# Later places in the order for the steps of ScalarE and VectorE that read a projection, the transposed maxima and the mixed values

## The reference

```
x = x + 0.5 * _L0_ffn_ref(_layernorm(x))    # 8 experts of 256, top 2, squared relu
x = x +       _L0_attn_ref(_layernorm(x))   # 32 heads of 32, output layer norm
x = x + 0.5 * _L0_ffn_ref(_layernorm(x))
x = x + 0.5 * _L1_ffn_ref(_layernorm(x))    # 8 experts of 512, top 2, capacity 640
x = x +       _L1_attn_ref(_layernorm(x))   # 16 heads of 64, biases on q, k, v
x = x + 0.5 * _L1_ffn_ref(_layernorm(x))
```

## Time and profile before

| | |
|---|---|
| median of three runs | 3482.12 us |
| the profiled execution, its own time | 3475.47 us |
| its span, first to last instruction | 3473.7 us |
| TensorE busy over the span | 3046.4 us (88%) |
| TensorE's weight loads | 1900.0 us (55%) |
| VectorE / ScalarE / GpSimd busy | 2161.3 / 1726.7 / 1745.8 us |
| mean granted clock of TensorE | 0.941 of full speed |

### The profile page before, as it was taken

How to read it: one execution, slowest core, us unless ns; L and a number is a source line. 1 busy time by engine, 2 the same in 40 slices (tenths; PEclk the granted TensorE clock), 3 DMA queues, 4 the chain that set the end, 5 groups by cost and what they waited for, 6 DMA issues and landing times. The chain is left out here.

```text
span 3473.7 us, 46628 instructions
## 1 busy us (share of the span) xinstructions
PE 3046.4 (88%) x16106; PEld 1900.0 (55%) x16106; DVE 2161.3 (62%) x4520; ACT 1726.7 (50%) x3306; POOL 1745.8 (50%) x1540
## 2 busy tenths in 40 slices
PE   7999999999999999979862849999999999999276
PEld 6884455454545455458752835555555555554165
DVE  5567666676666666746666425666766666666642
ACT  5555666666666666646540414344443444433032
POOL 0005877788787878840101724444444435444056
PEclk9999999999999999989985969999999999999578
DMA  2004334333333333300010434433434444433034
GB/s 88 1 19 92 86 81 93 74 82 85 81 86 87 83 86 78 74 25 16 13 41 24 82 89 100 92 90 85 104 89 92 98 95 95 98 85 68 25 69 73
DMA packets 182987, 254.00 MB, mean 73 GB/s; under 512 B 35904, under 2 KB 75584, under 8 KB 182208
## 3 DMA queue, kind: packets, MB, share of 16 engines
q1 hardware_dynamic: 168672, 240.19, 29.3%
q0 software_dynamic: 14080, 10.82, 2.3%
HBM read 33.44 MB, written 16.67 MB: 14 GB/s over the span
## 5 line engine op out<-in xcount | busy, mean ns | idle before, releaser
L1737 POOL TENSOR_TENSOR arena<-arena 128x512 f32<-128x512 f32 x1152 | 1439.8, 1276 | 866.7 <-ACT arena L1119 843.4
L780 PE MATMUL psum<-stack 96*128 96x512 f32 (+4 forms) x4096 | 1345.8, 442 | 70.0 <-DMA stack<-halves 42.3
L1375 DVE TENSOR_REDUCE top<-psum 128x1 f32<-128x512 f32 x1536 | 1002.0, 685 | 406.0 <-PE psum L780 402.0
L1119 ACT ACTIVATE arena<-psum 128x512 f32<-128x512 f32 x1536 | 866.3, 595 | 449.6 <-PE psum L780 438.2
L780 PEld LDWEIGHTS psum<-stack 96*128 96x128 f32 (+4 forms) x4096 | 707.3, 191 | 676.3 <-issue 353.5
L810 PE MATMUL psum<-arena,values 128*32 128x512 f32 (+1 forms) x3072 | 552.8, 613 | 0.0
L1706 POOL TENSOR_SCALAR rstd<-mv 128x4 f32<-128x4 f32 x56 | 12.6, 226 | 581.7 <-DVE mv L1241 579.9
L768 PE MATMUL psum<-xT,wqkv 128*128 128x512 f32 x512 | 268.2, 605 | 6.7 <-DVE arena L1420 3.0
L1407 DVE RECIPROCAL psum<-psum 128x128 f32<-128x128 f32 x256 | 226.4, 926 | 61.6 <-PE psum L840 61.6
L1082 ACT ACTIVATE halves<-psum,bqk 128x512 fp32r<-128x512 f32 x128 | 87.9, 687 | 308.3 <-PE psum L768 308.3
L1327 DVE SCALAR_TENSOR_TENSOR X<-psum,weight,X 128x128 f32<-128x128 f32 x512 | 144.0, 344 | 143.4 <-PE psum L747 143.3
(11 more groups left out here) (154 smaller groups left out, 3064.7 us busy)
## 6 DMA issues: line engine op xcount, KB each, us to landing
stack<-halves SPq DMA_DIRECT2D x768, 128.0 KB, 2.3
stack<-halves SPq DMA_DIRECT2D x384, 256.0 KB, 4.8
tokens<-xn SPq DMA_DIRECT2D x16, 256.0 KB, 2.4
sums<-X SPq DMA_DIRECT2D x16, 256.0 KB, 3.4
wqkv<-in_wg SPq DMA_DIRECT2D x16, 256.0 KB
wqkv<-in_wu SPq DMA_DIRECT2D x16, 256.0 KB
wqkv<-in_wd SPq DMA_DIRECT2D x16, 256.0 KB
wqkv<-in_w_qkv SPq DMA_DIRECT2D x2, 1536.0 KB, 9.8
```

Of the source, the lines that this page charges most:

```text
L780: ins = T_.matmul(bk, st[0:k, side, slot + h, cols], st[0:k, 1 - side, slot + h, :], start=r == 0, stop=r == len(PARTS[l]) - 1)
L1119: S_.activation(prob[l][tile % N_PROB][:, h, :], psum[:, bank[key], :], ACT.Exp, scale=scale).then_inc(released[bank[key]], 1)
L1375: give(V_.reduce_max(top[i][:, j:j + 1], psum[:, bank[key], :], AX.X), key)
L1737: ins = G_.tensor_tensor(to[:, h, :], old[:, h, :], prob[l][tile % N_PROB][:, h, :], ALU.add)
```

## The change

It does four things, all of them to the order and none to the arithmetic.

1. The step `project` stays as it is for TensorE. What ScalarE does of it is now the step `high`, 0.06 of a group later than TensorE's; what VectorE and SP do is now `low`, 0.11 later in attention 0 and 0.10 in attention 1.
2. `rows` (the transposed maxima) has three calls, one for each reader: TensorE works at the first, ScalarE at the second, VectorE and SP at the third.
3. `mix` has one call more in attention 0: ScalarE's spread moves one call on (3.85 to 3.96), TensorE's transposes back and VectorE's multiplication with them (to 4.07 and 4.19).
4. Smaller: the copy of a transposed norm (`xT`) is a step `fill` of its own, about 0.06 later; routing has one call more; the copy of a group's weighted values (the second call of `last`) moves by 0.04 in attention 0.

```
 WHEN = (
-    dict(project=(-0.11, 0.67), maxima=(0.97, 1.82), rows=(1.85, 1.85), probs=(2.21, 3.17),
-         last=(3.18, 3.24), mix=(3.51, 4.19), out=(4.24, 5.01), ahead=(-2.20, -0.56),
+    dict(project=(-0.11, 0.67), high=(-0.05, 0.73), low=(0.00, 0.78), maxima=(0.97, 1.82), rows=(1.87, 1.96),
+         probs=(2.21, 3.17), last=(3.18, 3.32), mix=(3.51, 4.30), out=(4.24, 5.01), ahead=(-2.20, -0.56),
...
             queue("project", (l, n), 3, 3, n)
+            queue("high", (l, n), 3, 3, n)
+            queue("low", (l, n), 3, 3, n)
             queue("maxima", (l, n), heads * TILES_B, heads * TILES_B, n)
-            queue("rows", (l, n), 1, 1, n)
+            queue("rows", (l, n), 3, 3, n)
             queue("probs", (l, n), (heads + 1) * TILES_B - 1, (heads + 1) * TILES_B, n)
-            queue("mix", (l, n), 6, 6, n)
+            queue("mix", (l, n), 6 + (l == 0), 6 + (l == 0), n)
...
-            def project(l, n):
+            def high_halves(l, n):
...
             def rows_of_maxima(l, n):
                 i, n_top, key = n % 2, HEADS[l] * TILES_B, ("top", l, n)
+                yield
...
-            def project(l, n):
+            def low_halves(l, n):
...
-            def project(l, n):
+            def fill_stack(l, n):
                 s, hv, st, width = n % N_STACK, halves[n % 2], stack[n % N_STACK], WIDTH[l]
-                yield
                 yield
```

More of the change, by code:

```diff
@@ L1038, in ahead, with fill @@
                 yield from normalise(("a", l, b), b)
+                yield
+            def fill(l, b):
                 fill_xt(("a", l, b))
@@ L1209, in experts1 @@
                 yield
-            play(order, dict(load0=load0, prepare0=prepare0, route=route, ahead=ahead, compute0=compute0,
-                             project=project, rows=rows_of_maxima, probs=probabilities, last=last_tile, mix=mix,
+            play(order, dict(load0=load0, prepare0=prepare0, route=route, ahead=ahead, fill=fill, compute0=compute0,
+                             high=high_halves, rows=rows_of_maxima, probs=probabilities, last=last_tile, mix=mix,
                              settle=settle, experts1=experts1))
@@ L1911, in _ @@
                 load(X[:, b * TILES_B:(b + 1) * TILES_B, :], x_v[b], got_x[b])
-            play(order, dict(load0=load0, load_attention=load_attention, project=project, rows=rows_of_maxima,
+            play(order, dict(load0=load0, load_attention=load_attention, low=fill_stack, rows=rows_of_maxima,
                              route=route, keep=keep, experts1=experts1))
```

31 lines of the change are left out of this document (24 added, 7 removed).

## The result

The changed kernel takes 3716.10 us (median of four runs, 3706.25 to 3718.09) against 3482.28 us of the kernel before on the same chip (3475.59 to 3482.63): a ratio of 1.0675, with a 95% interval of 1.0655 to 1.0694, or +234 us. Forecast were 3606 us, in a range of 3530 to 3650. The sign was right, the size was not.

The account below looks back on a forecast made before the run. The prediction took TensorE's order and its waits in the two attentions as the bound. It added 71 + 54 + 6 = 131 us to the profiled 3475.5 us, giving 3606 us, in a range of 3530 to 3650.

Parts of the forecast that it names:

- Part 1: Attention 1: k's halves come later, so the DMA landing TensorE waits for is 1.42 us later in 50 groups: 71 us.
- Part 2: Attention 0, behind q: the spread stands in front of the exponentials, about 0.85 us in each of 64 groups: 54 us.
- Part 3: Attention 0: k's low half, 2.5 us later, fits into 2.9 of room; a score bank freed later costs 6 us.
- Part 4: Possible gains: 6.8 us before the norm's transposes, about offset; routing and `fill` 0; ScalarE's shorter waits worth only TensorE's share.
- rival C: Both attentions: waits of 2 to 3 us per group lower TensorE's clock, 66 us more, 3672 us; chance 0.05.
- Rival B: Both attentions: not slower, as engines take ready work first and free banks earlier; 3460 us; chance 0.08.

Follow-up runs that it names:

- e1: The kernel before with only the high and low halves of attention 1 placed later (0.18 and 0.22 instead of 0.12): 3576.03 us, ratio 1.0305.
- e4: The kernel before with only the seventh call of `mix` in attention 0: ratio 1.0115.
- e11: The kernel before with the seventh call of `mix` in attention 0 and `last` at 3.18 to 3.32 instead of 3.18 to 3.24: ratio 1.0144.
- e2: The kernel before with only routing's steps spread over seven calls instead of six: 3536.07 us, ratio 1.0193.
- e6: The changed kernel with routing back on six calls and the transposed maxima of attention 1 back at one place: 3651.88 us, ratio 1.0482.
- e13: The kernel before with routing on seven calls and GpSimd's additions cut from 512 to 16 columns in two groups per batch: 3512.44 us, ratio 1.0082.
- e5: The kernel before with late halves in attention 1, plus two useless matmuls ahead of each wait for the landings there: 3569.54 us, ratio 1.0252.

## Why the prediction was wrong in size

**Part 1, right in mechanism and in size.** In the groups with P first, which is what was read, the exponential, the high and the low half were forecast 1.08, 1.58 and 2.74 us behind the start of the ten matmuls and came at 1.08, 1.57 and 2.75. With M first the exponential waits for its product until 1.54 and the high half is at 2.03, and the low half is at 2.75 all the same: the high half and the reduction ahead of it end together, at 2646.80. The weight load waited for the landing in 52 groups (50 before). At full clock the landings cost 73 us by the groups of e1, forecast were 71. That the shift adds up so well is in part luck, since some positions lose 1.1 us and one 2.0. What e1 measured beyond it, 46 of its 119 us, is the clock.

**Part 2, right in size, wrong in place.** 54 + 6 were forecast, 67 measured. I numbered ScalarE's exponentials off by one against TensorE's products: the one that the third product needs runs ahead of the high half of q, not behind the spread. The weight load behind q waits 0.42 and no matmul a microsecond. Of the 67 us, 24 are in the one group of eight with the output norm, where ScalarE waits for the later multiplication. In a plain group `mix` brings 0.38 of 0.82 us (e4); TensorE waits 0.3 us for an exponential there. The rest comes with the copy of the weighted values and the high half of k, which stand ahead of exponentials in the row of ten (e11, and the rows of place 2). That the sum was close is luck: it was forecast as the same 0.85 us in each of 64 groups.

**Part 3, right.** The late low half of k went into its room: TensorE waits 1.1 us in two waits for `stack` in 300 to 1450.

**Part 4 has the first step that failed: "Routing and `fill` move by a twentieth of a group: 0".** It cost some 65 us, 51 in attention 1 and 14 in the experts (e2, and by the medians e6 the other way). The twentieth is `fill`'s, and I took it for both. The calls of routing stand 0.30 of a group apart before and after, and the last one, with nearly all of VectorE's routing work in it, moved by a whole call, from 6.40 to 6.70. Past what it moved I didn't look: it changed sides with the first reciprocal, whose multiplication gives a bank back to q. Nor did I look at what GpSimd does beside the new place: the call takes twice as long there, and e13 puts two thirds of the 51 us on that. What makes up the 14 us in the experts was not tried.

**The clock is the second: the sum has no term for it.** It stood only in rival C, with a chance of 0.05, as an alternative to the forecast, when it is an addition to it. Half clock in attention 1 rose from 23 to 181 us, and by the groups of e1 it cost 46 us there; rival C had priced it at 66. The sentence in the earlier trace rows that a stretch with waits of 0.7 has a clock of 1.00 was true, and says nothing of waits of 2 to 3 us.

**Rival B, not slower.** ScalarE's waits for q and k did shrink, from 277.9 us to 118.8 in attention 1. TensorE got nothing of it, as the prediction's objection to B says.

**The sum, as measured.** Attention 1: 73 (landings) + 46 (clock, with the landings late) + 51 (routing, with its own clock) = 170 taken singly, 159 in the profile of the changed kernel; the 11 us between lie within what single profiles differ by. Attention 0: 67. Experts: 18, of which routing 14. Together 243 us in the profiles, 234 by the medians. The forecast of 131 and the two terms it lacked, 65 and 46, make 242.

## What to carry to other kernels

Where the order comes from a table and each engine keeps to it, count an edit by what each moved step passes, not by how far it moves: three tenths of a group, past one reciprocal and into GpSimd's additions, cost 65 us. A rival can be an addition: the late landings brought waits, and the waits brought half clock. A filler against it has a price of its own, so read the clock's cost from groups at full and at half clock in one trace. And test the opposite edit: projections 0.05 to 0.13 of a group earlier took the wait away and made the kernel 27 us faster.

## What the runs showed of the hardware

- VectorE's operations with two fp32 operands in SBUF (128x256) take 0.42 us alone and 1.39 us while GpSimd adds 128x512 in SBUF, six in 8.10 us; a 128x32 one takes 0.19 and 1.19. Reductions of the same call (0.42) and those that read PSUM (0.69) don't change; one scaling with a single operand in SBUF does (0.17 and 0.96). The Trainium skill ("SBUF — State Buffer", SBUF: two separate sides) says that a VectorE operation with two SBUF inputs and a GpSimd one that reads SBUF exclude each other for a whole instruction. The trace agrees: the 0.97 us more is less than the 1.35 of one addition, and in e13, where the additions are short, the operation takes 0.42. What this case adds is that a later place in VectorE's order put the call beside GpSimd's additions.
- TensorE's granted clock fell to 1.2 GHz for a part of the time when it stood still once per group of some 18 us for 2 to 3 us: 133 us of 1230 in e1 and 181 of 1270 in the changed kernel, against 23 of 1111 before, where the waits were 0.7 us. Two matmuls in the gap brought it back to 2.4 GHz for all but 24 us (e5). The Trainium skill ("TensorE: Matmul & The Clock Gate", Why this matters for your kernels) warns of idle gaps; the trace agrees. A group took 17.69 us at full clock and 19.35 with a granted clock of 0.91. TensorE was at work for most of the half clock: of its 181 us in the changed kernel only 24 lie in idle time of over 0.2 us. Filling the gap gave back 18 us by the medians, since the dummies cost an estimated 28.
